# Layer norm fused on VectorE in routing, the second combine weights on GpSimd, and the experts' stage reordered with its weight splits on GpSimd

## What is computed

```
xn = layernorm(x) * gamma + beta                       # per row of 256
x_unit = xn / max(norm(xn), 1e-12)
logits = (x_unit * scale) @ mu_unit                    # 256 rows x (16 experts x 16 slots)
dispatch = softmax(logits, over rows); combine = softmax(logits, over expert slots)
slot_in = dispatch^T @ xn
h = gelu(slot_in @ w1[e] + b1[e]);  slot_out = h @ w2[e] + b2[e]      # expert by expert
x = x + combine @ slot_out
```

## Time and profile before

| | us |
|---|---|
| Time, median of 3 runs (lowest, highest) | 1244.21 (1241.42, 1247.08) |
| The profiled execution: time, span | 1238.86, 1236.7 |
| `route`, about 986.6 to 1141 of the span | 154 |
| `experts`, about 1141 to 1194.7 | 54 |
| `combine`, about 1194.7 to 1236.7 | 42 |
| PE, DVE, ACT, POOL busy over the span | 1064.9, 920.8, 715.7, 438.3 |
| Mean granted clock of TensorE | 0.906 of 2.4 GHz |

### The profile page before, as it was taken

How to read it: one execution, slowest core, us unless ns; L and a number is a source line. 1 busy time by engine, 2 the same in 40 slices (tenths; PEclk the granted TensorE clock), 3 DMA queues, 4 the chain that set the end, 5 groups by cost and what they waited for, 6 DMA issues and landing times. The chain is left out here.

```text
span 1236.7 us, 28303 instructions
## 1 busy us (share of the span) xinstructions
PE 1064.9 (86%) x8053; PEld 1014.9 (82%) x8053; DVE 920.8 (74%) x2388; ACT 715.7 (58%) x2225; POOL 438.3 (35%) x753
## 2 busy tenths in 40 slices
PE   7779999999999997899999548888888747777998
PEld 6679999999999996899999547787887647676777
DVE  4567677777677765777777649989899769997656
ACT  4466666676666664333333237777777526566754
POOL 0223222223222220121212136666566466663015
PEclk9889999999999999899999859888888969889559
DMA  7578940000000000000000235444455000000113
GB/s 236 129 133 243 114 101 0 0 0 0 0 0 0 0 1 6 27 0 0 0 0 0 63 111 153 143 133 140 140 140 146 17 15 2 0 0 1 43 32 122
DMA packets 71574, 73.90 MB, mean 60 GB/s; under 512 B 23025, under 2 KB 63829, under 8 KB 71381
## 3 DMA queue, kind: packets, MB, share of 16 engines
q1 hardware_dynamic: 70692, 72.47, 23.4%
q10 hardware_dynamic: 816, 0.66, 0.2%
HBM read 41.52 MB, written 31.54 MB: 59 GB/s over the span
## 5 line engine op out<-in xcount | busy, mean ns | idle before, releaser
L776 POOL TENSOR_TENSOR att_prob<-att_ex,att_rinv 128x308 f32<-128x308 f32 x128 | 89.9, 702 | 216.1 <-DVE att_rinv L679 202.7
L1051 ACT ACTIVATE att_ex<-att_s_bank,att_mx 128x77 f32<-128x77 f32 x512 | 125.5, 337 | 30.9 <-DVE att_mx L1117 28.9
L1330 ACT ACTIVATE ffn_hid<-ffn_h_bank,ffn_b 128x256 f32<-128x256 f32 x128 | 60.8, 476 | 125.4 <-DVE ffn_hT_lo L1361 65.6
L638 ACT ACTIVATE att_ex<-att_s_bank,att_mx 128x77 f32<-128x77 f32 x512 | 125.0, 333 | 11.4 <-DVE att_mx L669 11.3
L1188 POOL TENSOR_TENSOR att_prob<-att_ex,att_rinv 128x256 f32<-128x256 f32 x128 | 79.1, 618 | 96.4 <-DVE att_rinv L1129 94.6
L702 DVE TENSOR_TENSOR att_pT_lo<-att_t_bank,att_pT_hi 128x512 fp32r<-128x512 f32 x128 | 88.3, 690 | 32.2 <-ACT att_pT_hi L616 31.8
L646 ACT ACTIVATE att_qT<-att_q_bank 128x256 f32<-128x256 f32 x128 | 49.2, 385 | 101.1 <-PE att_q_bank L496 100.0
L516 PE MATMUL att_s_bank<-att_keys,att_qT 128*128 128x154 f32 x512 | 95.0, 309 | 0.0
L616 ACT CAST att_pT_hi<-att_t_bank 128x512 fp32r<-128x512 f32 x128 | 75.0, 587 | 24.2 <-PE att_t_bank L526 19.3
L964 PE MATMUL att_s_bank<-att_ks,att_qs 100*128 100x154 f32 x256 | 54.6, 300 | 39.5 <-ACT att_ex L1051 32.3
L540 PE MATMUL att_o_bank<-att_pT_hi,att_vals_hi 128*128 128x256 f32 x256 | 83.0, 324 | 3.0 <-DVE att_oT_lo L683 2.0
(11 more groups left out here) (274 smaller groups left out, 4174.0 us busy)
## 6 DMA issues: line engine op xcount, KB each, us to landing
att_qs<-q_dram SPq DMA_DIRECT2D x96, 128.0 KB, 2.7
ks_dram<-att_zeros SPq DMA_DIRECT2D x16, 462.0 KB, 5.6
att_ks<-ks_dram SPq DMA_DIRECT2D x16, 462.0 KB, 5.0
all_x<-in_x SPq DMA_DIRECT2D x4, 1024.0 KB, 7.0
att_vd<-vd_dram SPq DMA_DIRECT2D x16, 256.0 KB
q_dram<-att_qT_hi SPq DMA_DIRECT2D x16, 256.0 KB, 2.1
q_dram<-att_qT_lo SPq DMA_DIRECT2D x16, 256.0 KB, 2.1
out<-comb_y SPq DMA_DIRECT2D x16, 256.0 KB, 2.1
```

What stands on the lines that cost most here:

```text
L638: last = nc.scalar.activation(ex[t % RING][:, r, :], s_bank[t % 2][:, r * SK:(r + 1) * SK], ACT.Exp, bias=mx[t % 2][:, r:r + 1])
L776: nc.gpsimd.tensor_tensor(out, e, w, ALU.mult).then_inc(p_ready, 1)
L1051: last = nc.scalar.activation(ex[t % RING][:, r, :], s_bank[t % 2][:, r * SK:(r + 1) * SK], ACT.Exp, bias=mx[t % 2][:, r:r + 1])
```

## The change

In `route`, POOL's `affine` and the plain `normalise` go. DVE now does xg = (x - mean) * gamma and xa = xg * rstd + beta with two `scalar_tensor_tensor` instructions of 128x256 each. `statistics(f+3)` moves behind the transposed x; the new `normalise(f+2)` stands behind the subtraction for dispatch. `weigh(f, 1)` leaves DVE: POOL does it as one product of 128x512, behind `inverse_deviation(f+3)` and ahead of `lengths(f+2)`.

In `experts` the loops are written out, `down` lags `up` by two experts (buffers of w2 and of the hidden values become three), and POOL casts and subtracts w1 and w2. POOL's queue is w1(0); w1(1), w2(0); w1(2), w2(1); w1(3), w2(2) and so on. `split_w1(e)` waits for both loads of expert e (`w_in`), and SP's condition for a load is unchanged.

```
@@ route, VectorE @@
+            def normalise(f, i):
+                dve.wait_ge(ln.rstd_ready, f + 1)
+                at_least(dve, ln.ready, NC * f)
+                for q in range(NC):
+                    nc.vector.scalar_tensor_tensor(xg[:, q, :], x_rows(st, f, q), ln.mean_var[:, q, 0:1], gamma[:, :],
+                                                   ALU.subtract, ALU.mult).then_inc(xg_ready, 1)
+                at_least(dve, xu_ready, NC * (f - 1))
+                at_least(dve, xas_ready, f - 1)
+                for q in range(NC):
+                    dve.wait_ge(xg_ready, NC * f + q + 1)
+                    nc.vector.scalar_tensor_tensor(xa[i][:, q, :], xg[:, q, :], ln.rstd[:, q:q + 1], beta[:, :],
+                                                   ALU.mult, ALU.add).then_inc(ln.ready, 1)
...
-                if later:
-                    ln.normalise(dve, f + 2, xg_ready, 1)
...
-                if latest:
-                    ln.statistics(dve, f + 3)
+                if later:
+                    normalise(f + 2, i)
...
                 if following:
                     transposed_x(f + 1, 1 - i)
+                if latest:
+                    ln.statistics(dve, f + 3)
                 if front:
                     weigh(f, 0)
                 if front:
                     invert(f, 1)
-                    weigh(f, 1)
@@ route, GpSimd @@
-            def affine(f, i):
...
+            def weigh(f):
+                wait_apart(poolt, rinv_ready, 2 * f + 2)
+                wait_apart(poolt, t_psum, 2 * f)
+                nc.gpsimd.tensor_tensor(weight[1][:, :, :], ex[1][:, :, :],
+                                        rinv[1][:, :].unsqueeze(2).to_broadcast([P, 2, ES]), ALU.mult).then_inc(weight_ready[1], 1)
...
                 if front:
                     split_x(f, i)
-                if later:
-                    affine(f + 2, i)
                 if latest:
                     ln.inverse_deviation(pool, f + 3)
+                if front:
+                    weigh(f)
                 if later:
                     lengths(f + 2)
@@ experts @@
+            for e in range(2, E):
+                sp.wait_ge(w2_lo, e - 1)
+                load_expert(sp, d, st, e, e % 2, w_in[e % 2])
...
+            for e in range(E + LAG):
+                if e < E:
+                    up(e)
+                if e >= LAG:
+                    down(e - LAG)
...
+        @block.gpsimd
+        def _(pool):
+            def split_w1(e):
+                i = e % 2
+                at_least(pool, w_in[i], 32 * (e // 2))
+                at_least(pool, h_psum, e - 1)
+                nc.gpsimd.tensor_copy(w1[i][0][:, :, :], w1_raw[i][:, :, :]).then_inc(w1_hi, 1)
+                pool.wait_ge(w1_hi, e + 1)
+                nc.gpsimd.tensor_tensor(w1[i][1][:, :, :], w1_raw[i][:, :, :], fp32_of(w1[i][0][:, :, :]), ALU.subtract).then_inc(w1_lo, 1)
+
+            def split_w2(e):
+                i, r = e % 2, e % RING
+                at_least(pool, o_psum, e - 2)
+                nc.gpsimd.tensor_copy(w2[r][0][:, :], w2_raw[i][:, :]).then_inc(w2_hi, 1)
+                pool.wait_ge(w2_hi, e + 1)
+                nc.gpsimd.tensor_tensor(w2[r][1][:, :], w2_raw[i][:, :], fp32_of(w2[r][0][:, :]), ALU.subtract).then_inc(w2_lo, 1)
+
+            split_w1(0)
+            for e in range(E):
+                if e + 1 < E:
+                    split_w1(e + 1)
+                split_w2(e)
```

More of the change, by code:

```diff
@@ L1777, in experts @@
 def experts(nc, d, st):
+    LAG, RING = 2, 3
     with ExitStack() as stack:
@@ L1799, in slots_of, with up @@
         def slots_of(e):
-            return st.slots[:, :, :, bass.ds(e * S, S)]
+            return st.slots[:, :, :, e * S:(e + 1) * S]
         @block.sync
         def _(sp):
[L1804 to L1807, removed]
+            for e in range(2, E):
+                sp.wait_ge(w2_lo, e - 1)
+                load_expert(sp, d, st, e, e % 2, w_in[e % 2])
+            for i in range(2):
+                sp.wait_ge(w_in[i], 32 * (E // 2 - 1))
         @block.tensor
         def _(pe):
-            def up(e, i):
+            def up(e):
+                i = e % 2
+                pe.wait_ge(w1_lo, e + 1)
                 pe.wait_ge(in_lo, e + 1)
@@ L1824, in down @@
                     for n, (a, b) in enumerate(PASSES):
-                        last = nc.tensor.matmul(o_bank[i][:, c * B * S:(c + 1) * B * S], w2[i][a][:, c * P:(c + 1) * P],
-                                                hT[i][b][:, :], start=n == 0, stop=n == 2)
+                        last = nc.tensor.matmul(o_bank[i][:, c * B * S:(c + 1) * B * S], w2[r][a][:, c * P:(c + 1) * P],
+                                                hT[r][b][:, :], start=n == 0, stop=n == 2)
                 last.then_inc(o_psum, 1)
[L1829 to L1833, removed]
             nc.tensor.transpose(b_bank[0:HID, 0:E], b_raw[:, 0:HID], st.ident[0:E, 0:E])
@@ L1851, in split_w2 @@
[L1851 to L1872, removed]
@@ L1874, in _, with hidden @@
-            split_inputs(0, 0)
-            split_w2(0, 0)
-            act.wait_ge(b_ready, 2)
-            batch_pairs(act, step)
+                nc.scalar.copy(xin[e % 2][0][:, :, :, :], slots_of(e)).then_inc(in_hi, 1)
+            def hidden(e):
+                act.wait_ge(h_psum, e + 1)
+                at_least(act, hid_lo, e - 1)
+                nc.scalar.activation(hid[e % 2][:, :], h_bank[e % 2][0:HID, 0:B * S], ACT.Gelu,
+                                     bias=b1[:, e:e + 1]).then_inc(hid_ready, 1)
@@ new lines, in outputs @@
+            def outputs(e):
+                act.wait_ge(o_psum, e + 1)
+                act.wait_ge(in_lo, e + 1)
+                for c in range(DC):
+                    nc.scalar.activation(st.slots[:, c, :, e * S:(e + 1) * S],
+                                         o_bank[e % 2][:, c * B * S:(c + 1) * B * S].rearrange("p (b s) -> p b s", b=B),
+                                         ACT.Identity, bias=b2[:, c, e:e + 1]).then_inc(out_stored, 1)
+            round_inputs(0)
+            act.wait_ge(b_ready, 2)
@@ L1879, in _, with split_inputs @@
+            for e in range(E + LAG):
+                if e + 1 < E:
+                    round_inputs(e + 1)
+                if e < E:
+                    hidden(e)
+                if e >= LAG:
+                    outputs(e - LAG)
         @block.vector
         def _(dve):
-            def split_inputs(e, i):
+            def split_inputs(e):
                 dve.wait_ge(in_hi, e + 1)
-                nc.vector.tensor_tensor(w1[i][1][:, :, :], w1_raw[i][:, :, :], fp32_of(w1[i][0][:, :, :]), ALU.subtract)
@@ L1905, in _, with split_hidden @@
-            split_inputs(0, 0)
-            split_w2(0, 0)
+            def split_hidden(e):
+                r = e % RING
+                dve.wait_ge(hid_ready, e + 1)
+                at_least(dve, o_psum, e - 2)
+                nc.vector.tensor_copy(hT[r][0][:, :], hid[e % 2][:, :]).then_inc(hid_hi, 1)
+                dve.wait_ge(hid_hi, e + 1)
+                nc.vector.tensor_tensor(hT[r][1][:, :], hid[e % 2][:, :], fp32_of(hT[r][0][:, :]), ALU.subtract).then_inc(hid_lo, 1)
+            split_inputs(0)
```

75 lines of the change are left out of this document (26 added, 49 removed).

## The result

The changed kernel takes 1280.05 us (median of 4 runs, 1277.91 to 1282.84) against 1244.45 (1241.42 to 1247.08): ratio 1.029, 95% interval 1.026 to 1.032. It is slower by 35.6 us; the forecast was slower by 46.5. The profiled execution took 1277.91 us with a span of 1276.1, against 1238.86 and 1236.7. The spans thus differ by 39.4 us, more than the medians. One source of such differences can be seen: the code ahead of `route` is the same in all kernels, yet route's first VectorE instruction starts anywhere between 987.2 and 993.3 us in the thirteen traces of this study. So a few us between two medians say little, and what follows rests on the lengths of steps and stages inside the traces.

What follows compares the result with a forecast made beforehand. Before, DVE bounds route and PE experts; after, closed chains through POOL's queue bind both. Route +21.1 and experts +25.4 give +46.5 on the median 1244.2: 1291 us, own bounds 1271 to 1309, with C 1264 to 1309.

Steps and rivals of the forecast that it cites:

- Route's closed chain: Route's step: DVE from unit to aggregates, POOL's rstd, weight and length, back to DVE's reciprocal; 10.19 us against 8.43.
- length to reciprocal 1.34: Route: from the start of POOL's length to DVE's reciprocal, 1.34 us of each step.
- the four scalar_tensor_tensor: Route, DVE's new instructions: 0.42 + 3 x 0.33 = 1.41 us a step, bounds 1.3 and 1.7.
- the pair of xu: Route, DVE: with only POOL's xaS_lo beside it, 1.63 us instead of 2.60, bounds 0.66 and 1.9.
- Route's sum: Whole route stage: 14 steps 140.3 us (+22.3), start -1.6, last batch +0.4; +21.1 us, bounds +7 to +31.
- Twelve of 10.19: Route: twelve of the 14 steps, between the first and the last, each cost 10.19 us.
- Experts: Experts stage: 4.98 us per expert from round trip, w1 and w2; 78.4 us against 53.0, +25.4, bounds +20 to +34.
- round trip: Experts: POOL's subtraction done, SP issues the loads, next use of the weights; 2.73 us exposed in each expert.
- B: Route: POOL's three pieces are not last, DVE bounds at 7.7 us a step, -10; total 1260; chance 0.10.
- C: Experts: the round trip is hidden, PE stays the bound at 3.05 us, route as forecast; total 1265; chance 0.08.
- D: Route: PE joins the chain, its clock staying at 1.2 GHz; 10.7 us a step, +7, total 1298; chance 0.10.
- E: Both stages: ready POOL instructions pass waiting ones; route by DVE's 7.7, experts by PE's 3.05; 1234 to 1237; chance 0.03.

Runs made afterwards that it cites:

- lengths_first: Changed kernel with POOL's order per step turned: split of x, weight of the step before, lengths(f+2), inverse deviation of f+3 last; 1308.95 us, ratio 1.053.
- best: As `lengths_first`, plus ACT's squares of f+2 ahead of its half-1 exponentials and experts' w1 and w2 loads under separate semaphores; 1263.86 us, ratio 1.018.
- weight_last: Changed kernel with POOL's weigh(f) moved from ahead of lengths(f+2) to behind it; 1278.43 us, ratio 1.028.

## Why the prediction was right

**Route's closed chain: shown.** The forecast put it together from DVE 6.28, POOL 1.53, weight 1.04, length to reciprocal 1.34, in all 10.19. The step above has 6.18 (to 1110.13), 1.49 (to 1111.62), 1.00 and 1.34, in all 10.01; the loop's mean is 10.06. Within DVE's part two terms were off: the four scalar_tensor_tensor take 1.59, not 1.41 (472 ns each against the 422 of the earlier trace rows, 0.40 between starts, not 0.33), and the pair of xu 1.40 and 1.65 in turn, not 1.63. That the part still came out is in part luck: the second, and POOL's start 0.1 sooner, make up for the first. The weight is 1.04 us, as scaled from the earlier trace rows. DVE's idle time of 2.5 is 2.2 to 2.3, where the forecast said. That the weight's place was part of the chain is shown by moving it (DVE's wait fell by 1.0), and that its neighbour matters by what xu then lost.

**Route's sum: too high, +21.1 against +14.7.** Of the 14 steps, forecast 140.3 and measured 134.8, the ten in the loop were right (101.9 and 100.6). The four that stand outside it were priced with a looped step's rows and took 0.6 to 1.8 less. "Twelve of 10.19" was the step that failed: two of the twelve are written out, at 9.19 and 9.30. The first, at 9.59, took 7.82, since its xu met no split either (0.74 for the pair), and the last 7.90 instead of 8.45. The start gave back 2.1, not 1.6, and the last batch cost nothing where 0.4 was set. These 6.4 us of route and 1.6 too much in experts, less the 0.9 that combine took though it was held untouched, make the 7.1 us between the forecast's 46.5 and the 39.4 of the spans. Most of the other 3.8, down to the 35.6 of the medians, is outside the mechanism: the forecast took the distance of the median from the profiled execution, 5.35, over to the changed kernel, where it was 2.1.

**Experts: +23.8 against +25.4, shown.** The round trip was 2.73 and is 2.66 in the mean (37.2 us in 14 waits). w1 takes 0.76, not 0.94, and w2 1.47, not 1.31: the cast and the subtraction of 64x256 are 0.39 and 0.72 when VectorE does nothing beside them (the last two experts) and 0.59 and 0.80 beside its split of the inputs. The errors cancel: 4.90 for 4.98. Separate semaphores for the loads bring all of it back, with POOL's work unchanged.

**The rivals.** B (relief in route) fell: three of POOL's pieces are last in every step. C (the round trip is hidden) is what separate loads made true, and only they. D (PE at the lower clock in route) fell here: the granted clock was 1.00. It came true in `lengths_first` and `best` (0.80 and 0.83 in the ten steps), where PE waited for the weight by 3 to 4 us a step instead of 1.3. E (a waiting POOL instruction is passed) fell in both stages: the weight starts behind rstd, and the cast of w2 behind that of w1, though its data were there.

The Trainium skill (SBUF — State Buffer, Who interferes with whom) has two kinds of VectorE instruction that contend with GpSimd: those in a two-port mode, which are shut out for the other's whole length, and those with two inputs in SBUF. The first agrees with xu in kind (401 ns alone, 1.04 us in the median of `weight_last`, beside the weight and the split), not in full size: beside the weight it lost 0.64 us of the 0.89 that the two lay together. The prediction noted the second and held that the four new instructions stand where POOL waits. That was so (472 ns in the median), until a run put POOL's products over them: then 1242 ns.

Not tried: statistics directly behind the fused norm, with nothing else moved. It would have told how much of the 0.5 us a step that the weight does not explain is their place.

## What to carry to other kernels

Before work is moved to a queue that is idle, write down what that queue's next instruction waits for, and what waits behind it: here GpSimd's queue closed a loop in each stage, and both together lost 36 us, in route with less work on both engines of the loop. A buffer that is reloaded should be asked for when its own last reader is done, not when the pair of them is. And work beside which another engine is held up is not hidden by being moved: look for the place where nothing runs that it holds up. Ask too who waits for it now: where PE did, its clock fell as well. Last, write out the looped steps of the kernel before and time that first, or its gain is put down to the change.

## What was not expected of the hardware

A product of 128x512 on GpSimd held up three kinds of VectorE instruction over SBUF, each by some three quarters of the time that the two lay together: xu (1037 ns beside the weight, 401 alone), the weights (a pair 0.62 alone, 1.62 beside 1.40 of the split) and scalar_tensor_tensor (a pair 0.86 alone, 2.42 with 2.1 of it beside two products). GpSimd loses little in return: the weight took 1.22 instead of 1.04.

The same step takes 0.8 to 0.9 us more in the loop, with waits on register values, than written out, in two different kernels (10.06 and 9.19; 8.68 and 7.90), and 0.2 in a third (8.31 and 8.14), where VectorE idled only 1.9 us in the ten looped steps (5.8 in those of before). What in the loop costs it is not shown beyond the handings over told above. For 16 steps the longer code cost nothing that could be seen.

TensorE's granted clock in the ten looped steps was lower the longer its longest single wait was: 1.00 at 1.3 us (the changed kernel), 0.92 at 2.0 (the kernel before, whose PE waits for xu), 0.90 at 2.6 (`weight_last`), 0.83 at 3.8 (`best`) and 0.80 at 4.2 (`lengths_first`). With the steps of before written out the longest was 1.2 us and the clock 1.00.
